# Attention layer on one Trainium2 core: accumulator copy, score shift and the sum of exponentials rearranged

## The reference

```
f = xf @ Wf + bf; g = xf @ Wg + bg; hh = xf @ Wh + bh      # 32, 32 and 256 columns
scores = einsum('bnd,bmd->bnm', g, f)
attn = softmax(scores, axis=-1)
o = einsum('bnm,bmc->bnc', attn, hh) @ Wo + bo
out = gamma * o + xf
```

## Time and profile before

| | us |
|---|---|
| median of 3 runs | 4687.89 |
| lowest and highest run | 4682.78, 4689.73 |
| span of the profiled execution | 4687.7 |
| layer 1 | from about 2617 to the end |

### The profile page before, as it was taken

The page is one execution under the profiler, slowest core; times in us unless marked ns, Lnnn a source line. Parts: engine busy times, 40 slices in busy tenths (PEclk is TensorE's granted clock), DMA queues, the critical chain, the costliest instruction groups (busy, mean ns, idle before and its releaser), DMA issues. The chain is left out here.

```text
span 4687.7 us, 79434 instructions
## 1 busy us (share of the span) xinstructions
PE 4400.2 (94%) x24320; PEld 3132.5 (67%) x24320; DVE 3877.6 (83%) x7295; ACT 3348.9 (71%) x5828; POOL 3672.9 (78%) x3476
## 2 busy tenths in 40 slices
PE   5899999999999999999998899999999999999998
PEld 3556565656565656565655578878878777878887
DVE  4899999899989998999998577777777777777775
ACT  5888889888889888988896355555555555555555
POOL 4898989898989898989897366667666676666666
PEclk7899999999999999999999799999999999999999
DMA  2011111111111111111101400040001300040000
GB/s 82 21 40 47 36 48 35 48 35 47 36 46 37 48 35 47 36 49 34 49 29 43 128 22 17 17 120 21 22 22 45 90 22 20 22 121 22 15 19 19
DMA packets 139380, 198.15 MB, mean 42 GB/s; under 512 B 18458, under 2 KB 106500, under 8 KB 138756
## 3 DMA queue, kind: packets, MB, share of 16 engines
q1 hardware_dynamic: 139012, 193.76, 13.0%
HBM read 114.02 MB, written 79.69 MB: 41 GB/s over the span
## 5 line engine op out<-in xcount | busy, mean ns | idle before, releaser
L1296 POOL TENSOR_TENSOR pl<-probs,ph 128x512 fp32r<-128x512 f32 x1024 | 1322.1, 1292 | 641.9 <-PE ps_o L1409 324.3
L748 POOL TENSOR_TENSOR dec<-dt,rates 128x384 f32<-128x384 f32 x1536 | 1512.6, 1015 | 250.4 <-ACT dt L634 194.7
L1502 ACT ACTIVATE ph<-ps_s 128x512 fp32r<-128x512 f32 x1024 | 613.4, 599 | 897.7 <-PE ps_s L1392 891.9
L1514 DVE TENSOR_REDUCE part_max<-ps_m 128x1 f32<-128x512 f32 x1024 | 689.5, 689 | 386.1 <-PE ps_m L1375 385.6
L1401 PE MATMUL ps_o<-ph,vh 128*128 128x512 f32 x2048 | 812.3, 397 | 19.8 <-ACT o_ch L1488 19.6
L1401 PE MATMUL ps_o<-ph,vl 128*128 128x512 f32 x2048 | 805.5, 393 | 0.0
L1543 DVE TENSOR_TENSOR ps_a<-probs,ps_a 128x512 f32<-128x512 f32 x992 | 681.5, 687 | 40.9 <-ACT probs L1504 35.4
L1409 PE MATMUL ps_o<-pl,vh 128*128 128x512 f32 x2048 | 634.9, 391 | 0.0
L1504 ACT ACTIVATE probs<-ps_s 128x512 f32<-128x512 f32 x1024 | 608.2, 594 | 0.0
L906 DVE SCALAR_TENSOR_TENSOR psS<-u,bc,psS 128x384 f32<-128x384 f32 x1024 | 599.2, 614 | 1.2
L915 DVE SCALAR_TENSOR_TENSOR y_tok<-psS,bc,y_tok 128x384 f32<-128x384 f32 x960 | 553.8, 607 | 4.5
(11 more groups left out here) (166 smaller groups left out, 7668.4 us busy)
## 6 DMA issues: line engine op xcount, KB each, us to landing
values_d<-hid SPq DMA_DIRECT2D x64, 512.0 KB, 4.1
xf<-in_x_dram SPq DMA_DIRECT2D x128, 128.0 KB
xb<-in_x_dram SPq DMA_DIRECT2D x128, 128.0 KB
residual_d<-xb SPq DMA_DIRECT2D x32, 512.0 KB, 2.7
vh<-values_d SPq DMA_DIRECT2D x32, 512.0 KB, 6.7
vl<-values_d SPq DMA_DIRECT2D x32, 512.0 KB, 7.7
res<-residual_d SPq DMA_DIRECT2D x32, 512.0 KB, 3.3
out_dram<-res SPq DMA_DIRECT2D x128, 128.0 KB
```

The lines of the kernel that those rows point to most:

```text
L748: last = nc.gpsimd.tensor_tensor(dec[:, q % RING, j - 1, :], dt[:, par, d, token_of(d, j), :], rates[:, d, n, :], ALU.mult)
L1296: nc.gpsimd.tensor_tensor(pl[:, m % DEPTH, :], probs[:, m % DEPTH, :], ph[:, m % DEPTH, :].bitcast(F32), ALU.subtract).then_inc(pl_ok, 1)
L1502: nc.scalar.activation(ph[:, m % DEPTH, :], ps_s[m % 2][:, :], ACT.Exp).then_inc(ph_ok, 1)
L1514: nc.vector.tensor_reduce(part_max[:, qt, kc:kc + 1], ps_m[r % 2][:, :], AX.X, ALU.max).then_inc(max_out, 1)
```

## The change

- ACT's copy of `ps_o[0]` is split off `take_sums` and stands at m = 1, between the exponentials of step 0 and of step 1. The copy of `ps_a` stays at m = 2. On PE, `values_high(c, 0, 0)` stands behind the scores and the maximum's matmuls of step 0.
- The shift: DVE computes minus the row maximum into `ps_t`, its rounded high part into column 96 and the rest into column 97 of `shift_hl` (three instructions on four elements for each partition, m = 26). PE transposes `shift_hl` by four transposes at m = 28, DVE copies rows 96 to 127 to `gq` at m = 28 (one instruction). `diag`, `max_hi`, `pick` and `row_max` are gone.
- The sum: four transposes of `sums` fill `ps_t`, DVE sums each 128 columns (one `tensor_reduce` over 512 elements), writes the reciprocal into `ps_t` and the product with gamma to `total`.

```diff
-MAX_REDUCE, MAX_DIAGONAL, MAX_SPREAD, MAX_ROWS = MAX_STEPS, MAX_STEPS + 1, MAX_STEPS + 2, MAX_STEPS + 3
+MAX_REDUCE, MAX_SPREAD, MAX_ROWS = MAX_STEPS, MAX_STEPS + 2, MAX_STEPS + 2
...
             def spread_max(c):
-                pe.wait_ge(max_ok, 4 * c + 2)
+                pe.wait_ge(max_ok, 4 * c + 3)
                 for qt in range(QT):
-                    mm = pe.matmul(ps_m[0][:, qt * P:(qt + 1) * P], ones[:, :], diag[:, qt, :], start=True, stop=True)
+                    mm = pe.transpose(ps_m[0][:, qt * P:(qt + 1) * P], shift_hl[:, qt, :], ident[:, :])
                 mm.then_inc(bcast_ok, 1)
...
                 for qt in range(QT):
-                    mm = pe.matmul(ps_t[:, qt:qt + 1], sums[:, qt * P:(qt + 1) * P], ones[:, 0:1], start=True, stop=True)
+                    mm = pe.transpose(ps_t[:, qt * P:(qt + 1) * P], sums[:, qt * P:(qt + 1) * P], ident[:, :])
                 mm.then_inc(sum_full, 1)
...
                     ending = m == KEYS - 1
-                    values_high(c, m, 0)
+                    if m > 0:
+                        values_high(c, m, 0)
...
                         if m == MAX_SPREAD:
                             spread_max(c + 1)
+                    if m == 0:
+                        values_high(c, m, 0)
...
-            def take_sums(c):
+            def take_o(c):
                 act.wait_ge(lo_done[0], KEYS * c + KEYS + DEPTH)
                 act.wait_ge(turn_full, 2 * c + 2)
                 nc.scalar.activation(o_ch[:, 0, :], ps_o[0][:, :], ACT.Copy).then_inc(o_out[0], 1)
+
+            def take_sums(c):
+
                 act.wait_ge(acc_ok, KEYS * c + KEYS + DEPTH)
...
+                    if m == 1 and at != "first":
+                        take_o(c - 1)
                     if m == AHEAD and at != "first":
                         take_sums(c - 1)
...
+            def shift_parts(c):
+                row, hi, lo = ps_t[:, 0:QT], shift_hl[:, :, 96], shift_hl[:, :, 97]
+                dve.wait_ge(max_out, KEYS * (c + 1) + 2)
...
+                nc.vector.tensor_reduce(row, part_max[:, :, :], AX.X, ALU.max, negate=True).then_inc(max_ok, 1)
+                dve.wait_ge(max_ok, 4 * c + 1)
+                nc.vector.tensor_copy(hi.bitcast(F32R), row).then_inc(max_ok, 1)
+                dve.wait_ge(max_ok, 4 * c + 2)
+                nc.vector.tensor_tensor(lo.bitcast(F32R), row, hi, ALU.subtract).then_inc(max_ok, 1)
+            def shift_rows(c, par):
+                dve.wait_ge(bcast_ok, c + 1)
+                nc.vector.tensor_copy(gq[par][96:P, :], ps_m[0][96:P, :]).then_inc(max_ok, 1)
...
-                nc.vector.reciprocal(total[:, :], ps_t[:, 0:QT]).then_inc(total_ok, 1)
-                dve.wait_ge(total_ok, 2 * c + 1)
-                nc.vector.tensor_scalar(total[:, :], total[:, :], gamma_sb[:, 0:1], None, ALU.mult).then_inc(total_ok, 1)
+                nc.vector.tensor_reduce(total[:, :], ps_t[:, :].rearrange("p (q k) -> p q k", q=QT), AX.X,
+                                        ALU.add).then_inc(total_ok, 1)
+                dve.wait_ge(total_ok, 3 * c + 1)
+                nc.vector.reciprocal(ps_t[:, 0:QT], total[:, :]).then_inc(total_ok, 1)
+                dve.wait_ge(total_ok, 3 * c + 2)
+                nc.vector.tensor_scalar(total[:, :], ps_t[:, 0:QT], gamma_sb[:, 0:1], None, ALU.mult).then_inc(total_ok, 1)
...
                         if m == MAX_REDUCE:
-                            finish_max(c + 1, 0, 1 - par)
-                        if m == MAX_DIAGONAL:
-                            finish_max(c + 1, 1, 1 - par)
+                            shift_parts(c + 1)
                         if m == MAX_ROWS:
-                            finish_max(c + 1, 2, 1 - par)
-                            finish_max(c + 1, 3, 1 - par)
+                            shift_rows(c + 1, 1 - par)
```

More of the change, by code:

```diff
@@ L1212, in layer1 @@
         part_max = sb("part_max", [P, QT, PER_IMAGE])
[L1213 to L1216, removed]
+        shift_hl = sb("shift_hl", [P, QT, P])
         res = sb("res", [P, 2, QT, C])
@@ L1279, in _ @@
         def _(pool):
[L1281 to L1286, removed]
+            nc.gpsimd.memset(f_st[96:P, :, :].bitcast(F32), 0.0).then_inc(const_ok, 1)
+            pool.wait_ge(const_ok, 1)
+            nc.gpsimd.memset(shift_hl[:, :, :], 0.0).then_inc(const_ok, 1)
+            pool.wait_ge(const_ok, 2)
+            nc.gpsimd.memset(f_st[96:98, :, :].bitcast(F32), 1.0).then_inc(const_ok, 1)
             pool.sem_inc(pl_ok, DEPTH)
@@ L1422, in turn_half @@
                         pe.wait_ge(o_out[cb], c + 2)
-                    pe.wait_ge(total_ok, 2 * c + 2)
+                    pe.wait_ge(total_ok, 3 * c + 3)
                 else:
@@ L1470, in _ @@
             spread_max(0)
-            pe.wait_ge(const_ok, 4)
+            pe.wait_ge(const_ok, 3)
             for m in range(AHEAD):
@@ L1506, in _ @@
             chunks(act, body)
+            take_o(B * PER_IMAGE - 1)
             take_sums(B * PER_IMAGE - 1)
@@ L1514, in reduce_max @@
                 nc.vector.tensor_reduce(part_max[:, qt, kc:kc + 1], ps_m[r % 2][:, :], AX.X, ALU.max).then_inc(max_out, 1)
[L1516 to L1533, removed]
+            def shift_parts(c):
+                row, hi, lo = ps_t[:, 0:QT], shift_hl[:, :, 96], shift_hl[:, :, 97]
+                dve.wait_ge(max_out, KEYS * (c + 1) + 2)
+                if not (exact(c) and c == 0):
+                    dve.wait_ge(turn_out, QT * (c - 1) + QT)
+                    dve.wait_ge(bcast_ok, c)
+                nc.vector.tensor_reduce(row, part_max[:, :, :], AX.X, ALU.max, negate=True).then_inc(max_ok, 1)
[6 more added lines that the diff above has]
+                nc.vector.tensor_copy(gq[par][96:P, :], ps_m[0][96:P, :]).then_inc(max_ok, 1)
             def add_keys(c, m):
@@ L1560, in write_out @@
                 if half == 0:
-                    dve.wait_ge(total_ok, 2 * c + 2)
+                    dve.wait_ge(total_ok, 3 * c + 3)
                     dve.wait_ge(res_ok, QT * c + QT)
@@ L1598, in _ @@
                 reduce_max(0, r)
-            dve.wait_ge(const_ok, 4)
-            for what in range(4):
-                finish_max(0, what, 0)
+            dve.wait_ge(const_ok, 3)
+            shift_parts(0)
+            shift_rows(0, 0)
             chunks(dve, body)
```

## The result

| | before | after |
|---|---|---|
| median, us | 4688.8 | 4613.4 |
| lowest and highest run, us | 4682.8, 4690.2 | 4608.6, 4615.3 |
| span of the profiled execution, us | 4687.7 | 4612.5 |
| ratio of the times | | 0.9837 (95%: 0.9823 to 0.9851) |

The change makes the kernel 1.6% faster; forecast was 4618, the range 4608 to 4637. Further executions of the kernel before, measured beside the experiments, have a median of 4686.0 to 4686.2 us, so the gain is between 73 and 75 us against the 70 of the sum.

A forecast was written before the change was run, and what follows sets the result against it. PE was taken to bound the kernel, busy 98% in layer 1's steady chunks. The terms 17.4 + 22.0 + 13.6 + 17.6 + 1.8 - 0.4 - 2.0 = 70.0 us, off 4687.7, gave 4618 us, range 4608 to 4637.

The forecast's parts named there:

- the three turns: Chunk ends turning to a new image: two lose 0.46 us each waiting for queries, the third gains 1 us (0 to 3).
- The spread and the diagonals: The shift on PE: shorter spread gains 17.4 us, vanished waits for DVE's diagonals 22.0 us, first chunk 1.8 us.
- The sum: Four transposes on PE gain 0.44 us in each of 31 chunks, 13.6 us; DVE's added reduction stays hidden.
- The end of a chunk: PE's stalls for ACT's accumulator copy go in 28 chunks, 17.5 us; with the turns to a new image 17.6 us.
- Loop jumps: At 13 chunk ends PE's jump back in code is no longer hidden: 0.15 us each, 2.0 us back.
- Tail: At the very end the sum's reduction on DVE isn't covered: a loss of 0.4 us.
- Sum: All terms together: 70.0 us off the span of 4687.7 us, giving 4618 us, -1.5%.
- Rival 1: Stalls return at the next link, DVE's copy of the second half: 15 us back, 4633 us; chance 0.17.
- Rival 2: DVE's small instructions wait for POOL, so the factor comes late: 46 us back, 4664 us; chance 0.05.
- rival 3: PE's clock falls around the added transposes: up to 105 us lost, 4723 us, slower; chance 0.03.
- rival 4: ACT's time without instructions at jumps moves, PE stalls at more chunk ends: 18 us back, 4636, to 78; chance 0.04.

The follow-up runs named there:

- copy_behind: The changed kernel with DVE's copy of the second accumulator half behind its two maximum reductions of step 0 instead of ahead of them: 4664.5 us, ratio 0.9956.
- act_only: The changed kernel with PE's order in step 0 as before, so that only ACT's copy is moved ahead: 4620.3 us, ratio 0.9858.
- turn_early: The changed kernel with the first half of the output's transposes in step 3 instead of step 4: 4654.7 us, ratio 0.9935.

## Why the prediction was right

The mechanism was right, and nearly every term; the term for the three turns failed.

- **The spread and the diagonals.** Forecast 17.4 + 22.0 + 1.8 = 41 us, alone 40.1. In each chunk 0.54 or 1.77 us, against 0.56 and 1.78. In the first chunk spread to scores takes 1.95 us (2641.47 to 2643.42), where it took 3.71.
- **The sum.** Forecast 13 us, alone 11.4; 0.47 us a chunk against 0.44. The slack for the factor was forecast as 0.65 and is 0.67 us.
- **The end of a chunk.** Forecast 17.6, alone 15.7. The slack of DVE's copy was forecast at 0.18 us and is 0.18 from its end to the matmul; the weight load, which the forecast left out, already waits for it. Two sizes were off. The restart behind a wait gives another 0.1 us a chunk, 3 us. And the step on the three turns failed: I took them at -0.9 + 1 us. Against ordinary chunk ends, which give 0.46 us each, that is 1.3 us given back. From copy to copy, the steps there last 16.9 us more than ordinary ones in the profile after (63.68, 62.40 + 67.49, and 66.32 us against 60.74 each). Before it was 10.9 us (63.78, 65.43 + 67.59, and 64.53 against 62.31, 125.82 and 62.31). So they gave back 6 us, 4.7 more than I took; against the second profile of the kernel before, whose turns cost 13.0 us, it is 4 us, 2.6 more. I had priced the two value matmuls that now come behind the queries, but not that the queries come later: their matmuls start 6.5 and 6.9 us after the issue, where it was 6.05 and 6.1. So the waits for them went from 1.2 and 1.9 us to 2.7 and 3.8, more than the 1.0 us by which PE comes earlier. Why they come later isn't shown. Behind the second of these waits PE ran at a granted clock of 0.66 for 5 us, where before it was 1.00 after the shorter wait.

```profile
4119.00:4124.00 5.00, 4.67 (x13) 3.70 (x14) 2.71 (x5) 1.09 (x2) 0.08 (x1) 0.66 0.49 160
```

That is 0.34 x 5 = 1.7 us lost.

- **Loop jumps.** I took 2 us back, and nothing shows: inside the loops, chunk ends with and without a jump are mostly 60.72 to 60.76 us apart.
- **Tail.** Forecast 0.4 us lost. From the sum's first matmul to the transposes it is 2.01 us instead of 1.68, so 0.3. From there to the end another 0.4 us went, which I can't explain.
- **Sum.** 70 + 3 + 2 - 4.7 = 70 us of layer 1, and its profiles give 69 against before and 71 against before again. That the errors of +5 and -5 cancel is luck. The rest of the 73 to 75 us between medians isn't told apart from the scatter of layer 0, so the time is 5 us under the forecast for no shown reason. The base of the sum was also slightly off: the profiled execution's own time is 1.9 us over its span, as the runs show (4614.4 for 4612.5), not 0.2; this is common to both kernels and cancels.

Rival 1 named the right next link, but PE was not held up there; `copy_behind` shows its price. Rival 2 fell by the 0.22 us of the product, rival 3 by the clock of 1.00 with twelve transposes. Of rival 4 a trace is there: PE's gap at the second turn is still 5.2 us where it was 6.0, and PE has no other gap without a releaser.

## What to carry to other kernels

When one engine sets the pace, price each of its small groups from start to start and each wait from the point where its next instruction could have started, and then work out, in the same units, by how much the next link is early: here 0.18 and 0.67 us. Neither held PE up, but the first was closer than it looked, since the weight loads come ahead of their matmuls: read their waits too. Moving a copy one slot ahead in its engine's queue can remove a whole wait. When an engine runs faster through a place, look at which transfers were just in time there: at the turns PE came 1.0 us earlier and waited 1.5 and 1.9 us longer for the queries, and issuing them ahead of one part of the keys and values took both waits away.

## What the runs showed of the hardware that I had not expected

- A matmul that waited costs 0.1 us more than its wait: the next one starts 0.34 us later, not 0.23. It goes with a weight load that starts only together with its matmul (both at 3862.00 before the change, both at 3817.41 in `act_only`). Where the load waited but still started 0.12 us ahead of its matmul (3812.52 and 3812.64), nothing was lost.
- After a wait of 3.8 us PE's granted clock was 0.66 over 5 us, partly at 1.2 GHz, so the wait cost more than its length; after one of 1.9 us in the same place of the kernel before it was 1.00. The length alone doesn't decide it: after 2.7 us at the first turn of the changed kernel it was 1.00, and after 2.4 us at the same turn of `turn_early` 0.66:

```profile
3145.40:3150.40 5.00, 5.00 (x15) 4.02 (x16) 3.19 (x5) 1.09 (x2) 1.81 (x2) 0.66 0.57 184
```

- Transposes of 128 x 128 f32 cost 0.11 us each in a longer group (twelve in 1.23 us), four cost 0.35.
- PE's time without an instruction at the second turn was 3.7 to 5.2 us in seven kernels with a DMA share of 0.87 or more there, and 2.3 us in the one with 0.04.
